# A graph network with residual layernorm: nested Ifs for unused units, a ring of six in the first row stage, and the layernorm chunks spread over five stages

## The chip, the cores and the metric

One core of a Trainium2 chip. The metric is the device time of one launch in microseconds (us), the median of several runs.

## The reference

Inputs: `x` (50000 rows of 128), `src` and `dst` (25000 edges, sorted by `dst`), `edge_attr_16` (25000 by 16), four weight matrices and biases. A layer of edge convolution is `segment_sum(concat(h[src], edge_attr) @ W + b, dst) / max(count, 1)`; layer k takes the concatenated outputs of all layers before it as `h`:

```python
h = _edge_conv(x, src, dst, edge_attr, W0, b0, denom)
outputs = [h]
for W, b in ((W1, b1), (W2, b2), (W3, b3)):
    cat = jnp.concatenate(outputs, axis=1)
    outputs.append(_edge_conv(cat, src, dst, edge_attr, W, b, denom))
x = _layernorm(x + outputs[-1], axis=-1)
```

## The kernel before

The work is linear, so the kernel first sums the rows of `x` over the edges of each destination (a "rank"), 128 edges at a time, and then multiplies the sums once with products of the weights (the product steps, L1234 to L1247 on VectorE, L1709 to L1716 on TensorE, at most `CIT` = 25 steps of 8 blocks). Results are written to `z_of_nodes` for the final sum and to two tables in memory, `h_rows` and `part_rows`. Only a part of the ranks has sources that are themselves destinations; those are listed, and the higher layers are computed for the listed ranks alone:

- **A round** (`round_`, three of them) goes over the list of sources in groups of two blocks of 128: GpSimd gathers two blocks of rows (L674), VectorE builds one-hot matrices (L1407, in `EC`, memory of its own for six groups), TensorE multiplies (L1749, L1755), VectorE adds the result to `UT` (L1423, L1424). GpSimd may be 12 blocks ahead.
- **The first row stage** (`first_rows`) goes over the listed ranks in pairs of blocks. For a pair GpSimd gathers two blocks of 2 KB rows of `part_rows` (L688, "wide"), VectorE casts the node numbers out of them (L1466), makes the pair's rows (L1470 to L1472), GpSimd gathers the nodes' rows of `x` (L666), VectorE adds them (L1459, `add_x`), SyncE stores the parts (L501) and the rows (L496). Pairs share a ring of three places in `SX`: `gather_wide(q)` waits for the rows and the part store of pair q-3. `XLAG` = 1: the node gather of pair q is issued after the wide gather of pair q+1.
- **The second row stage** (`second_rows`) loads the parts back in batches of ten blocks (L515) and makes rows from them (L1486); **the last** (`last_rows`) does so once more, normalises and scatters the rows to the output (L711).

How many blocks there are depends on the input. The rounds' blocks are cut into nine units at `RUNITS` = 0, 60, 66, 70, 76, ..., the rows' at `LUNITS` = 0, 20, 40, 50, 60, 70, ...; unit 0 always runs, and each other one stands in an If of its own on every engine, one behind the other. At the end of a row unit GpSimd and SyncE wait until the last three part stores have landed.

The layernorm of all nodes is 30 **chunks** of 13 rows per partition: SyncE loads a chunk of `x` and one of `z_of_nodes` (L466, L469) into rings of three and two, VectorE adds them and takes statistics (L1386, L1371 to L1379), and, for the chunk before, the scale and shift (L1392, L1393); ScalarE scales (L862) and stores. `load_chunk(c)` waits for the store of chunk c-3. Each transfer is 832 KB (852 thousand bytes), three to a chunk. `LROUND` = 10, 10, 10 puts ten chunks into the first unit (30 groups) of each round, at the groups that `spread_chunks` gives (1, 4, 7, ...); `LSTAGE` = 0, 0 puts none into the row stages. Each engine's order is written out by hand.

Of the kernel before, what the change touches and what calls it, by code (L numbers as in the profile page):

```python
# [7 lines left out]
T = (E + P - 1) // P  # L8
# [38 lines left out]
LROUND = (None, 10, 10, 10)  # L47
LSTAGE = (None, 0, 0)
# [24 lines left out]
AX = mybir.AxisListType  # L73

# [29 lines left out]
def gnn_kernel(nc, x, dst_t, prev_t, src_t, dst_rows, ea, wt, wr, vt, v3, part_of_block, unit_table, out):  # L104
# [11 lines left out]
    with ExitStack() as ctx:  # L116
# [14 lines left out]
        LG = SX[:, :].rearrange("p (j w) -> p j w", w=4 * D)  # L131
        LROWS = SX[:, 0:2 * LB * D].rearrange("p (b j c) -> p b j c", b=2, c=D)
# [176 lines left out]
        wide_here = [sem(f"wide_here{j}") for j in range(3)]  # L309
        x_here, parts_out = ([sem(f"{n}{j}") for j in range(3)] for n in ("x_here", "parts_out"))  # L310
# [45 lines left out]
        def _(e):  # L356
# [122 lines left out]
            def l_pairs(body, tail=None):  # L479
                for u in range(NU):  # L480
                    def unit():
                        for q in range(LUNITS[u] // 2, LUNITS[u + 1] // 2):
                            body(q)
                        if tail:
                            tail(LUNITS[u + 1] // 2)
                    if u:
                        with e.If(n_l > u):
                            unit()
                    else:
                        unit()  # L490
# [7 lines left out]
            def first_pair(q):  # L498
                r = q % 3
                e.wait_ge(s["z_added"], q + 1)  # L500
                e.dma_start(plrows[:, 2 * q:2 * q + 2, :], LG[:, 2 * r:2 * r + 2, D:3 * D]).then_inc(parts_out[r], 16)  # L501
                if 2 * q not in LUNITS:
                    store_rows(1, q - 1)
                if q in SPLACE[1]:
                    chunk(SBASE[1] + SPLACE[1].index(q))

            def first_end(q):
                store_rows(1, q - 1)
                for p in range(q - 3, q):
                    e.wait_ge(parts_out[p % 3], 16 * (p // 3 + 1))  # L510
# [6 lines left out]
            def l_batches(part, here, done):  # L517
                for u in range(NU):
                    lo, hi = LUNITS[u] // LB, (LUNITS[u + 1] + LB - 1) // LB
                    def unit():  # L520
                        for t in range(lo, hi):
                            done(t, min((t + 1) * LB, T) // 2)
                            if t + 2 < hi:
                                load_batch(t + 2, part, here)
                            for w in range(u + 1, NU):
                                if LUNITS[w] <= (t + 2) * LB < LUNITS[w + 1]:
                                    with e.If(n_l > w):
                                        load_batch(t + 2, part, here)
                    if u:
                        with e.If(n_l > u):  # L530
                            unit()
                    else:
                        unit()
# [31 lines left out]
        def _(e):  # L565
# [72 lines left out]
            for i in range(CIT):  # L638
                with e.If(n_s > i):
                    for b in (0, 1):  # L640
# [4 lines left out]
                        for j in range(CG):  # L645
                            c = q * CG + j
                            g.indirect_dma_start(ZF, bass.IndirectOffsetOnAxis(ap=sum_rows[:, c:c + 1], axis=0), HS3[:, b, j, 3 * D + 1:4 * D + 1], None,  # L647
                                                 bounds_check=last_sum, oob_is_err=False).then_inc(scat[b], 16)
            n_e, n_l, n_q = list_counts(e, (UNITS_R, UNITS_L, PAIRS))
# [8 lines left out]
            def gather_x(q):  # L658

                r = q % 3  # L660
                if q >= 3:
                    e.wait_ge(s["z_added"], q - 2)
# [6 lines left out]
            def round_(k, table, last):  # L669
# [7 lines left out]
                for u in range(1, NU):  # L677
                    with e.If(n_e > u):
                        unit(u)

            def gather_wide(q):
                r = q % 3
                if q >= 3:
                    e.wait_ge(rows_made[1], q - 2)
                    e.wait_ge(parts_out[r], 16 * (q // 3))
# [1125 lines left out]
```

## Time and profile before

| | us |
|---|---|
| median of 3 runs (lowest, highest) | 1434.44 (1433.83, 1435.81) |
| the profiled execution | 1429.92 |
| its span | 1427.8 |
| busy: TensorE matmul, VectorE, ScalarE, GpSimd | 564.5, 769.2, 444.0, 802.0 |
| counts of gathers and scatters: L647, L674 (each round), L688, L666, L711 | 144, 70, 60, 60, 60 |
| mean of one scaling on ScalarE, L862 | 0.479 |

The profile is of one execution; its engines' busy times are over the whole span and overlap. The steps priced below are read from stretches of it.

### The profile page before, as it was taken

To read this page: it belongs to the slowest core of one execution; us is meant where nothing else is said; L and a number is where in the kernel's file an instruction comes from. 1 tells how busy PE (TensorE), PEld (TensorE's weight loads), DVE (VectorE), ACT (ScalarE), POOL (GpSimd) and SP (SyncE) were. 2 spreads that over 40 slices of the span, in tenths; PEclk is the share of its full clock that TensorE was granted. 3 is DMA by queue.
4 is the path that set the end of the run, shared out by engine and by line. 5 is a ranking of instruction groups with operands and counts; after the bars stand their busy time and mean duration, and the time that the engine had idled before them with its cause. 6 is when DMAs were issued, how large, how long until landed. Compare 5 with 4: busy or idle time off the path is not lost.

```text
span 1427.8 us, 15526 instructions
## 1 busy us (share of the span) xinstructions
PE 564.5 (40%) x3020; PEld 429.8 (30%) x3020; DVE 769.2 (54%) x2933; ACT 444.0 (31%) x1066; POOL 802.0 (56%) x766
## 2 busy tenths in 40 slices
PE   2454542666657567773544200000254502544000
PEld 1443442444444234442444100000144401544000
DVE  7765557788763533322888321211377745875630
ACT  7543452122323234432355000000144401543440
POOL 6886665245424466666766265655376505663376
PEclk9555665556668888887677555555556666676555
DMA  2667879811105677777677255655657757674311
GB/s 57 230 218 246 295 225 324 257 35 38 27 14 195 203 254 253 245 256 242 240 268 283 73 173 143 179 155 155 179 194 278 273 146 234 249 255 142 117 53 38
DMA packets 157618, 265.66 MB, mean 186 GB/s; under 512 B 22672, under 2 KB 91367, under 8 KB 157472
## 3 DMA queue, kind: packets, MB, share of 16 engines
q1 hardware_dynamic: 112128, 149.57, 31.0%
q0 software_dynamic: 26240, 59.55, 15.3%
q10 hardware_dynamic: 19104, 54.92, 10.1%
q8 instruction: 52, 0.85, 0.3%
q14 instruction: 94, 0.77, 0.2%
HBM read 114.39 MB, written 149.75 MB: 185 GB/s over the span
## 4 chain that ended last, share of the span: by engine, by line
DVE 28%; issue 19%; DMA 19%; PE 14%; POOL 9%; ACT 5%; another core or an unknown queue 2%; SPq 2%; DVEq 2%; POOLq 0%; ACTq 0%
DMA area<-z_of_nodes 5%; DMA SX<-part_rows,nlo 5%; POOL out_rows L711 4%; ACT area L862 3%; DVE stat L1371 3%; DVE area L1199 3%; PE hp L1716 3%; DMA out_rows<-area 2%; DVE area L1386 2%; PE segp L1628 2%; DVE area L1219 2%; DVE area L1125 2%; PE segp L1716 2%; POOL SX L688 2%
## 5 line engine op out<-in xcount | busy, mean ns | idle before, releaser
L631 POOL DMA_INDIRECT G<-x_in,srci x196 | 223.5, 1140 | 157.0 <-PE segp L1628 82.2
L647 POOL DMA_INDIRECT z_of_nodes<-area,sum_rows x144 | 142.0, 986 | 104.6 <-issue 50.5
L1749 PE MATMUL segp<-ZERO 128*128 128x384 f16 (+1 forms) x54 | 26.3, 486 | 352.9 <-DVE EC L1407 335.3
L862 ACT ACTIVATE area<-area,shift,rs 128x128 f32<-128x128 f32 x390 | 153.3, 479 | 21.3 <-DVE shift L1393 19.8
L855 ACT ACTIVATE sd<-dev,eps 128x13 f32<-128x13 f32 x30 | 9.2, 306 | 459.5 <-DVE dev L1379 429.2
L674 POOL DMA_INDIRECT G<-part_rows,s0r x70 | 78.7, 1125 | 87.1 <-DMA part_rows<-UT 50.3
L1749 PEld LDWEIGHTS segp<-ZERO 128*128 128x128 f16 x54 | 6.9, 127 | 357.0 <-DVE EC L1407 338.5
L674 POOL DMA_INDIRECT G<-part_rows,previ x70 | 79.1, 1130 | 51.0 <-issue 36.5
L674 POOL DMA_INDIRECT G<-h_rows,dsti x70 | 78.8, 1126 | 41.6 <-DVE UT L1423 23.4
L688 POOL DMA_INDIRECT SX<-part_rows,nlo x60 | 60.8, 1014 | 70.1 <-issue 28.9
L1755 PE MATMUL segp<-G,EC 128*128 128x128 f32 (+1 forms) x432 | 88.1, 371 | 28.8 <-DMA G<-part_rows,previ 10.3
L1755 PEld LDWEIGHTS segp<-G,EC 128*128 128x128 f32 x432 | 88.0, 287 | 34.0 <-DMA G<-part_rows,previ 12.2
L837 ACT ACTIVATE area<-segp,zero,inv 128x512 f32<-128x512 f32 x72 | 54.4, 776 | 135.0 <-PE segp L1716 56.3
L1628 PEld LDWEIGHTS segp<-SX,G 128*128 128x128 f32 x392 | 91.2, 316 | 11.5 <-ACT SX L778 3.6
L711 POOL DMA_INDIRECT out_rows<-UT,idx x60 | 59.9, 998 | 60.1 <-ACT UT L887 42.1
L1628 PE MATMUL segp<-SX,G 128*128 128x128 f32 x392 | 90.5, 402 | 4.9 <-ACT SX L778 3.2
L789 ACT ACTIVATE UT<-segp,UT 128x1 f32 x56 | 14.6, 261 | 231.2 <-PE segp L1628 191.7
L1755 PEld LDWEIGHTS hp<-G,EC 128*128 128x128 f32 x408 | 83.2, 286 | 6.4 <-issue 2.7
L1755 PE MATMUL hp<-G,EC 128*128 128x128 f32 (+1 forms) x408 | 82.6, 370 | 3.7 <-issue 2.6
L1386 DVE TENSOR_TENSOR area<-area 128x1664 f32<-128x1664 f32 x30 | 56.8, 1894 | 45.5 <-DMA area<-z_of_nodes 41.9
L1371 DVE BATCH_NORM_STATS2 stat<-area 128x6 f32<-128x128 f32 x390 | 78.4, 278 | 1.0
L1466 DVE CAST sum_rows<-SX 128x2 uint32<-128x2 f32 x30 | 6.1, 204 | 129.2 <-DMA SX<-part_rows,nlo 129.2
(392 smaller groups left out, 1608.8 us busy)
## 6 DMA issues: line engine op xcount, KB each, us to landing
part_rows<-area SPq DMA_DIRECT2D x36, 1024.0 KB
z_of_nodes<-ZERO ACTq DMA_DIRECT2D x28, 1024.0 KB
area<-x_in SPq DMA_DIRECT2D x30, 832.0 KB
area<-z_of_nodes SPq DMA_DIRECT2D x30, 832.0 KB
out_rows<-area ACTq DMA_DIRECT2D x30, 832.0 KB
part_rows<-ZERO SPq DMA_DIRECT2D x56, 256.0 KB
h_rows<-area SPq DMA_DIRECT2D x36, 258.0 KB
listed_parts<-SX SPq DMA_DIRECT2D x30, 256.0 KB, 2.6
```

The lines of the kernel that those rows point to most:

```text
L631: g.indirect_dma_start(G[:, slot, 0:D], None, x, bass.IndirectOffsetOnAxis(ap=srci[:, c:c + 1].bitcast(u32), axis=0), bounds_check=last_no ...
L647: g.indirect_dma_start(ZF, bass.IndirectOffsetOnAxis(ap=sum_rows[:, c:c + 1], axis=0), HS3[:, b, j, 3 * D + 1:4 * D + 1], None, bounds_che ...
L674: g.indirect_dma_start(G[:, n % GS, 0:W1 if k == 1 else D], None, table, bass.IndirectOffsetOnAxis(ap=take[k - 1][:, n:n + 1], axis=0), bo ...
L688: g.indirect_dma_start(LG[:, 2 * r + w, :], None, TT, bass.IndirectOffsetOnAxis(ap=wide_row[:, b:b + 1], axis=0), bounds_check=last_row, o ...
L711: g.indirect_dma_start(out, bass.IndirectOffsetOnAxis(ap=node_u[:, b:b + 1], axis=0), UT[:, b * D:(b + 1) * D], None, bounds_check=last_no ...
L837: a.activation(HS3[:, b, j, PARTS], PBANK[j][:, :], ACT.Identity, bias=zero1[:, 0:1], scale=inv[:, g * CG + j:g * CG + j + 1]).then_inc(s[ ...
L862: last = a.activation(XL[:, b, k], XL[:, b, k], ACT.Identity, bias=shift[:, b, r:r + 1], scale=rs[:, b, r:r + 1])
L1371: last = v.bn_stats(stat[cols, b, r, :], src_[cols, r * D:(r + 1) * D])
L1386: lnk(v.tensor_tensor(XL[:, b, :], XL[:, b, :], ZL[:, c % ZRING, :], ALU.add))
L1628: t.matmul(SG[q][:, bass.ds(w, P)], G[:, slot, 0:D], S[:, slot, :], start=False, stop=j == hi - 1).then_inc(s["summed"], 1)
L1716: t.matmul(PBANK[j][:, 0:3 * D], UT[:, (g * CG + j) * P:(g * CG + j + 1) * P], M[:, :], start=False, stop=True).then_inc(s["p_mm"], 1)
L1755: last = t.matmul(bank[:, bass.ds(at_, width)], OH[:, g % OHG, j, w * P:(w + 1) * P], G[:, slot, first:first + width], start=False, stop=j ...
```

## The change

- `nested(e, count, u, end, body)` puts the If of unit u+1 inside that of unit u, behind its body. It takes the place of the rows of Ifs for the round units, row units and product steps on GpSimd, ScalarE, VectorE, TensorE and, for the row units, SyncE. SyncE's counted loop over the product steps stays.
- The first row stage has a ring of six (`WRING`), pairs 3 to 5 of it in `ECS_`, where the one-hots are (`wide_slot`); `XLAG` is 2, and `add_x` follows three pairs behind (`ADDLAG`) instead of one. The semaphores `x_here` are six that the first part of the kernel used, with their count added. VectorE now also waits at a row unit's end for the last six part stores.
- The 30 chunks: 8 in round 1, 4 in the first row stage, 8 in round 2, 2 in the second row stage, 8 in round 3. SyncE issues the loads of a chunk of the first row stage three pairs before VectorE's place for it.

```diff
-LROUND = (None, 10, 10, 10)
-LSTAGE = (None, 0, 0)
+LROUND = (None, 8, 8, 8)
+LSTAGE = (None, 4, 2)
-XLAG = 1
+XLAG = 2
+WRING = 6
+ADDLAG = 3
+def nested(e, count, u, end, body):
+    if u < end:
+        with e.If(count > u):
+            body(u)
+            nested(e, count, u + 1, end, body)
+        LE = ECS_[:, 0:6 * 4 * D].rearrange("p (j w) -> p j w", w=4 * D)
+        wide_slot = lambda r: LG[:, 2 * r:2 * r + 2, :] if r < 3 else LE[:, 2 * r - 6:2 * r - 4, :]
...
+        x_here = [gat[0], gat[1], gat[2], gat[4], gat[5], gat[6]]
+        X_BEFORE = 32 * (UNITS // 2)
...
             def first_pair(q):
-                r = q % 3
+                for i, place in enumerate(SPLACE[1]):
+                    if max(place - ADDLAG, 0) == q:
+                        chunk(SBASE[1] + i)
+                r = q % WRING
                 e.wait_ge(s["z_added"], q + 1)
-                e.dma_start(plrows[:, 2 * q:2 * q + 2, :], LG[:, 2 * r:2 * r + 2, D:3 * D]).then_inc(parts_out[r], 16)
+                e.dma_start(plrows[:, 2 * q:2 * q + 2, :], wide_slot(r)[:, :, D:3 * D]).then_inc(parts_out[r], 16)
                 if 2 * q not in LUNITS:
                     store_rows(1, q - 1)
-                if q in SPLACE[1]:
-                    chunk(SBASE[1] + SPLACE[1].index(q))
...
             def gather_wide(q):
-                r = q % 3
-                if q >= 3:
-                    e.wait_ge(rows_made[1], q - 2)
-                    e.wait_ge(parts_out[r], 16 * (q // 3))
+                r = q % WRING
+                if q >= WRING:
+                    e.wait_ge(rows_made[1], q - WRING + 1)
+                    e.wait_ge(parts_out[r], 16 * (q // WRING))
...
             def l_units(unit):
-                unit(LUNITS[0] // 2, LUNITS[1] // 2)
-                for u in range(1, NU):
-                    with e.If(n_l > u):
-                        unit(LUNITS[u] // 2, LUNITS[u + 1] // 2)
+                own = lambda u: unit(LUNITS[u] // 2, LUNITS[u + 1] // 2)
+                own(0)
+                nested(e, n_l, 1, NU, own)
...
             def first_rows(lo, hi):
-                for q in range(lo, hi + 1):
+                for q in range(lo, hi + ADDLAG):
...
-                    if q > lo:
-                        add_x(q - 1)
+                    if q - ADDLAG >= lo:
+                        add_x(q - ADDLAG)
+                for q in range(hi - WRING, hi):
+                    e.wait_ge(parts_out[q % WRING], 16 * (q // WRING + 1))
+                e.sem_inc(s["tick"], 1)
```

## Rows read from the trace of the kernel before

**Rows 1.** Windows: from:to, us, PE PEld DVE ACT POOL busy (x), PEclk, DMA, GB/s

```profile
666.00:796.00 130.00, 62.30 (x315) 57.53 (x315) 99.73 (x418) 49.05 (x127) 78.89 (x71) 0.69 0.69 241
810.00:874.80 64.80, 0.00 (x0) 0.00 (x0) 16.19 (x72) 0.00 (x0) 40.62 (x40) 0.50 0.57 162
874.80:939.80 65.00, 0.00 (x0) 0.00 (x0) 12.48 (x60) 0.00 (x0) 40.02 (x41) 0.50 0.57 162
939.80:974.40 34.60, 0.00 (x0) 0.00 (x0) 6.37 (x30) 0.00 (x0) 20.18 (x21) 0.50 0.53 152
974.40:1011.30 36.90, 0.00 (x0) 0.00 (x0) 6.50 (x30) 0.00 (x0) 20.25 (x20) 0.50 0.55 141
1156.30:1182.00 25.70, 0.00 (x0) 0.00 (x0) 15.96 (x60) 0.00 (x0) 0.00 (x0) 0.50 0.87 242
1420.50:1427.80 7.30, 0.00 (x0) 0.00 (x0) 0.00 (x0) 0.00 (x0) 0.00 (x0) 0.50 0.00 0
```

**Rows 2.** Timeline of VectorE, chunks: start, us, instruction, [idle before, releaser]

```profile
679.68 1.89 DVE L1386 TENSOR_TENSOR area<-area 128x1664 f32<-128x1664 f32 x1 [12.27 <-DMA area<-z_of_nodes]
...
774.77 1.89 DVE L1386 TENSOR_TENSOR area<-area 128x1664 f32<-128x1664 f32 x1 [1.79 <-DMA area<-z_of_nodes]
...
1017.39 1.89 DVE L1386 TENSOR_TENSOR area<-area 128x1664 f32<-128x1664 f32 x1
...
1052.17 1.88 DVE L1386 TENSOR_TENSOR area<-area 128x1664 f32<-128x1664 f32 x1
...
1117.72 1.89 DVE L1386 TENSOR_TENSOR area<-area 128x1664 f32<-128x1664 f32 x1 [2.07 <-DMA area<-z_of_nodes]
...
1128.01 1.89 DVE L1386 TENSOR_TENSOR area<-area 128x1664 f32<-128x1664 f32 x1 [0.87 <-DMA area<-z_of_nodes]
...
1133.54 0.17 DVE L1393 SCALAR_TENSOR_TENSOR shift<-dev,rs 128x13 f32<-128x13 f32 x1
...
1216.99 1.89 DVE L1386 TENSOR_TENSOR area<-area 128x1664 f32<-128x1664 f32 x1
...
1296.43 1.89 DVE L1386 TENSOR_TENSOR area<-area 128x1664 f32<-128x1664 f32 x1 [3.40 <-issue]
```

**Rows 3.** Chain of waits, VectorE's skips after round 1: start, us, what

```profile
795.76 2.29 issue
...
804.08 3.39 issue
```

**Rows 4.** Chain of waits, GpSimd after the first row stage: landing, longest skip

```profile
1008.82 2.48 DMA listed_parts<-SX
...
1014.88 5.81 issue
```

**Rows 5.** Timeline of VectorE, first instructions after the stages' ends

```profile
807.63 0.29 DVE L1529 TENSOR_TENSOR RX<-RX,RZ 80x128 f32<-80x128 f32 x1 [12.24 <-issue]
...
1014.99 0.26 DVE L1556 TENSOR_SCALAR wlo<-nodec 128x196 f32<-128x196 f32 x1 [6.20 <-issue]
...
1156.23 5.34 DVE L1486 SCALAR_TENSOR_TENSOR UT<-UT,nh,SX 128x128 f32<-128x128 f32 x20 [8.63 <-issue]
...
1326.62 0.24 DVE L1392 RECIPROCAL rs<-sd 128x13 f32<-128x13 f32 x1 [9.54 <-issue]
```

**Rows 6.** Timeline of GpSimd, a unit's end in the first row stage

```profile
860.24 0.99 POOL L688 DMA_INDIRECT SX<-part_rows,nlo  x1 [1.75 <-DVE rela L1472]
...
867.05 1.08 POOL L666 DMA_INDIRECT G<-x_in,sum_rows  x1 [1.91 <-DVE sum_rows L1466]
...
874.82 1.00 POOL L688 DMA_INDIRECT SX<-part_rows,nlo  x1 [5.38 <-issue]
```

**Rows 7.** The page's rates of all DMA, 40 equal slices

```profile
GB/s 57 230 218 246 295 225 324 257 35 38 27 14 195 203 254 253 245 256 242 240 268 283 73 173 143 179 155 155 179 194 278 273 146 234 249 255 142 117 53 38
```

**Rows 8.** Chain of waits, one wide gather and one batch load

```profile
854.89 4.08 DMA SX<-part_rows,nlo
...
1165.45 5.16 DMA SX<-listed_parts
```

More of the change, by code:

```diff
@@ L479, in l_pairs, with unit @@
             def l_pairs(body, tail=None):
[L480 to L486, printed above, removed]
-                        with e.If(n_l > u):
-                            unit()
-                    else:
-                        unit()
+                def unit(u):
+                    for q in range(LUNITS[u] // 2, LUNITS[u + 1] // 2):
+                        body(q)
+                    if tail:
+                        tail(LUNITS[u + 1] // 2)
+                unit(0)
+                nested(e, n_l, 1, NU, unit)
             def store_rows(k, q):
@@ L517, in l_batches, with unit @@
             def l_batches(part, here, done):
-                for u in range(NU):
+                def unit(u):
                     lo, hi = LUNITS[u] // LB, (LUNITS[u + 1] + LB - 1) // LB
[L520 to L533, printed above, removed]
+                    for t in range(lo, hi):
+                        done(t, min((t + 1) * LB, T) // 2)
+                        if t + 2 < hi:
+                            load_batch(t + 2, part, here)
+                        for w in range(u + 1, NU):
+                            if LUNITS[w] <= (t + 2) * LB < LUNITS[w + 1]:
+                                with e.If(n_l > w):
+                                    load_batch(t + 2, part, here)
+                unit(0)
+                nested(e, n_l, 1, NU, unit)
             def second_batch(t, end):
@@ L637, in _, with scatter_step @@
             g.memset(HS3[:, :, :, 4 * D + 3:5 * D + 1], 0.0).then_inc(s["tail_zero"], 1)
-            for i in range(CIT):
-                with e.If(n_s > i):
+            def scatter_step(i):
                     for b in (0, 1):
@@ L893, in _ @@
             l_unit(0)
-            for u in range(1, NU):
-                with e.If(n_l > u):
-                    l_unit(u)
+            nested(e, n_l, 1, NU, l_unit)
         @block.vector
@@ L1352, in _, with step @@
             edge_low(1)
[L1353 to L1360 removed]
+            def step(i):
+                scale_products(i)
+                if i + 2 < CIT:
+                    edge_rest(i + 2)
+                    edge_low(i + 2)
+                else:
+                    e.sem_inc(s["ecs_full"], 1)
+            for i in range(3):
+                with e.If(n_s > i):
+                    step(i)
                 if i == 1:
@@ L1441, in round_ @@
                 unit(0)
-                for u in range(1, NU):
-                    with e.If(n_e > u):
-                        unit(u)
+                nested(e, n_e, 1, NU, unit)
                 e.wait_ge(first_added[k], n_g)
@@ L1449, in l_units @@
             def l_units(unit):
-                unit(LUNITS[0] // 2, LUNITS[1] // 2)
-                for u in range(1, NU):
-                    with e.If(n_l > u):
-                        unit(LUNITS[u] // 2, LUNITS[u + 1] // 2)
+                own = lambda u: unit(LUNITS[u] // 2, LUNITS[u + 1] // 2)
+                own(0)
+                nested(e, n_l, 1, NU, own)
             def add_x(q):
-                r = q % 3
-                e.wait_ge(x_here[r], 32 * (q // 3 + 1))
-                own = LG[:, 2 * r:2 * r + 2, 2 * D:3 * D]
+                r = q % WRING
@@ L1767, in _ @@
                 unit(0)
-                for u in range(1, NU):
-                    with e.If(n_e > u):
-                        unit(u)
+                nested(e, n_e, 1, NU, unit)
 def kernel(x, src, dst, edge_attr_16, L0_gnn_W0, L0_gnn_b0, L0_gnn_W1, L0_gnn_b1, L0_gnn_W2, L0_gnn_b2, L0_gnn_W3, L0_gnn_b3):
```

86 lines of the change are left out of this document (42 added, 44 removed).

## The prediction

> **What bounds the kernel now.** I read the page's table of busy shares first: no engine is over 56% busy, so there is no single bottleneck and each stage has to be priced alone. The table of windows [rows 1] splits the second half of the span: list rounds (the first is its first line), row stages between them, a tail. In the round VectorE is the busiest engine, 99.7 of 130 us, with DMA at 0.69. In the first row stage GpSimd carries it: each unit of ten pairs takes 64.8 or 65.0 us, of which 40 gathers are 40.6 us busy, while VectorE works 16.2 us.
>
> The timeline of VectorE [rows 2] shows what paces a round. Nine gaps between chunks take the 95.1 us from 679.68 to 774.77, 10.6 us each, and the last of these chunks begins after a wait for a z load. That is a loop: statistics, ScalarE's scaling of the chunk before, the store, and only then SyncE's load into the freed buffer. Between two chunks stand three groups of the round.
>
> The chain of waits [rows 3, 4] shows the third thing: the gaps between stages. After round 1 VectorE does nothing from 795.8 to 807.5 us but pass the If of each of the six units that this input does not use; four of those jumps are long, 2.3 to 3.4 us, the first and the last are shown. GpSimd does the same after the first row stage, 5.8 us for the longest. VectorE's own rows [rows 5] give 12.2 us for this end and 6.2, 8.6 and 9.5 us for the others.
>
> **The change part by part.** (By the counts of gathers and scatters on the page, 70, 60 and 144, the input runs 3 of 9 round units, 4 of 9 row units and 18 of 25 product steps.)
>
> *Nested units.* Six or five skipped Ifs in a row become one jump to the end. One long jump is 2.3 to 3.4 us on VectorE and up to 5.8 us on GpSimd [rows 3, 4]; with the 0.5 us before it I put 3.3 us. At the five places that lie on the chain:
> - end of round 1: 12.2 us [rows 5] becomes 3.3, minus 9. VectorE's index work before the first wide gather moves up with it; GpSimd issued its last gather of the round before that and has nothing else to wait for.
> - end of the first row stage: GpSimd resumes at 1011.3 us, when the last parts have landed, and is past its skips at 1020.7, a microsecond before the first gather of round 2 [rows 4]. With one jump it would be there at 1015. But VectorE is next late: it now also waits for those parts at the end of a unit, then has its one jump (about 3 us) and 1.2 us of index work, so 1015.6. Minus 5.
> - end of round 2, 8.6 us [rows 5]: minus 5.5. End of round 3, 9.5 us: minus 6.
> - after the last scatter the span runs on for 7.3 us with no engine busy [rows 1], part of it landing, part GpSimd's five skips: minus 2.
>
> At the end of the product steps the same saving on VectorE and TensorE is worth nothing: SyncE's loop there is a counted one and is not changed, and the first chunk waits 12.3 us for its z load, until 679.68 [rows 2]. After the second row stage the skipped bodies are short and VectorE shows no gap. Sum: minus 27.5, bounds minus 20 (the jump as long as GpSimd's 5.8 us at three places) and minus 31 (every jump 2.3 us).
> The trace agrees here with the Trainium skill, "Runtime: NRT & Kernel Launch", section "Instruction fetch mechanics": a taken branch to code outside the small window of fetched instructions has to fetch it before anything runs. By that rule the nested jump still pays one fetch, and never none; a sum with the gap gone entirely would be 15 us lower, and I do not take it.
>
> *Rounds with 8 chunks for 10.* In the first unit (30 groups) a chunk now follows every 3.75 groups; the first and last places (groups 1 and 28) stay. If the loop of loads went on setting the pace, a round would lose two chunks of 10.6 us, 21.1 us. If VectorE alone set it, it would lose the work of two chunks, 5.65 us each from L1386 to L1393 (1128.01 to 1133.7, [rows 2]), 11.3 us. The truth lies between, because a gap now holds a chunk and about four groups: 5.65 plus 4 x 1.4 us is 11.3 us (the gap from 1117.72 to 1128.01 less the chunk and the 0.87 us of waiting leaves 3.8 for three groups, 1.3 each; I add a little for the groups that wait on TensorE), a little over 10.6. Round 1: nine gaps are 95.1 us, seven of 11.3 are 79: minus 16. Round 2: the first two gaps (1017.39 to 1052.17, 34.8 us, late gathers and one stall) stay and get 2.5 us more for their extra groups, the other seven (75.8 us, to 1128.01) become five of 11.3: minus 17. Round 3 likewise, the last seven gaps are 79.4 us (1216.99 to 1296.43) and become 56.5: minus 20, of which I take 18 because one stall in it may stay. Sum minus 51, bounds minus 34 and minus 64. GpSimd's 70 gathers at 1.3 us are 91 us, so it does not become the bound of a round of 112.
>
> *First row stage, six pairs in flight.* Removed: the waits for a ring of three, about 1.7 us at every second pair, and 1.9 us before the last node gather of a unit, which comes too soon behind its wide one [rows 6]. With XLAG 2 there are 7.8 us between them, and a wide gather lands in about 4 [rows 8]. What remains is GpSimd's own pace: four indirect DMAs a pair at 1.3 us (1.0 busy and 0.3 between), 5.2 us, and the drain at a unit's end, 5.4 us [rows 6], that the change keeps (both engines wait for all parts). A ten-pair unit so takes 57.4 us for 65.0, a five-pair unit 31.4 for 34.6 (939.8 to 974.4) and, at the end, 34 for 36.9 [rows 1].
> *Four chunks moved in.* All four stand in the first unit (pairs 1, 3, 6, 8). VectorE has room: 4 x 5.65 us beside 16.2 us of work in some 60. What has less is the DMA. The unit moves at 162 GB/s with a share of 0.57 [rows 1], 10.5 MB; four chunks add 4 x 2.56 MB. That makes 20.7 MB in 57 us, 360 GB/s, and no slice of the page's line of GB/s is over 324 [rows 7]. So the DMA ends this unit: 20.7 MB at 300 GB/s (between the 242 of [rows 1] and the 324) is 69 us. I take 68, plus 3 on before. The other units keep minus 7.6, minus 3.2 and minus 2.9. Stage: minus 11. Bounds: minus 25 (the DMA hides, GpSimd's pace alone, and a few drains overlap) and plus 14 (it runs at 260 GB/s, and each chunk's 5.65 us holds back a part store and with it a wide gather).
> The Trainium skill speaks against this part, "DMA: Bandwidth & Descriptors", section "Issuing engines are not separate DMA queues": all queues end on the same 16 engines, so moved loads are not free beside gathers; its table of specifications names about 358 GB/s for HBM per core. By that figure alone, an estimate, the unit would be DMA-bound at 58 us, near GpSimd's 57; no stretch of this trace is that fast, and the sum keeps to the 300.
> Added instructions: a wait of VectorE at each unit's end, behind which only the next unit's first cast is queued, and that needs a wide gather that GpSimd issues after the same landing: nothing. SyncE's chunk loads now stand three pairs early and wait for the store of a chunk; behind them wait part stores. I follow them through: load 10 frees at about 24 us after the stage's start, when the first part is due anyway; so 2 to 3 us, within the above.
>
> *Second row stage, two chunks moved in.* It takes 25.7 us at a DMA share of 0.87 [rows 1], its batch loads 5.2 us each [rows 8]. Two chunks add 5.1 MB, 17 us at 300 GB/s, and 11.3 us of VectorE, which idles for 10 of 26 us. SyncE, at pair 7, waits for the store of a chunk that is scaled only from pair 2 on (5.65 us of VectorE, 13 scalings of 0.48 us by the page's line of L862, and the store's landing), some 14 us later, and holds back the load of the fourth batch. By each count it ends 9 to 17 us later; I take plus 11 (bounds plus 5 and plus 17).
>
> *The rest*: half of the ring in the one-hots' memory, shared semaphores, the other shapes of loops change no instruction on the chain: 0 (bounds minus 1 and plus 2).
>
> Sum: minus 27.5, minus 51, minus 11, plus 11 is minus 78.5. The profiled execution took 1429.9 us, so 1351.4; the median of before is 4.5 us above its profiled one, so about 1356.
>
> **The rivals.**
> 1. *The moved chunks eat the ring's gain.* First stage plus 14, second plus 17, rounds minus 34 because the load loop, VectorE and TensorE's slow groups couple. With the jumps: 1434.4 - 27.5 - 34 + 14 + 17 = 1404; halfway between the forecast and that, 1380, is its likelier time. For: DMA 0.87 in the stretches where only loads run. Against: the rounds' waits before chunks are for loads [rows 2], and these go.
> 2. *Everything overlaps better*: rounds minus 63, first stage minus 22, second plus 6, jumps minus 29: 1326. For: VectorE's own work would allow it. Against: TensorE's granted clock is 0.69 in the round [rows 1], nearer its lower level of 1.2 GHz than 2.4, and groups in series wait for its matmuls.
> 3. *The nested bodies cost a jump when they are entered.* If nesting puts each body out of line, every executed If pays a jump on the engine that walks it. On VectorE that is 15 product steps, 2 entries in each of three rounds and 3 in each of three row stages, 30 entries. At the 3.4 us of the dearest VectorE jump that is 102 us against a gain of 78.5: 1458, slower. It decides from 2.6 us an entry. Against it: now an entered body follows with no gap, and nothing in the source moves it.
> 4. *The change does not do what it says*: nested Ifs leave one jump per level; the jumps' 27.5 us stay, 1383.
>
> **How the numbers follow.** Forecast 0.55; rival 1 0.2; rival 2 0.12; rival 4 0.08; rival 3 0.05. A change of under 0.2% is what a measurement of this kernel cannot tell from none. Forecast, rivals 1, 2 and 4 are all faster, save a sliver. Faster 0.94, same 0.01, slower 0.05. The likeliest own range is 1340 to 1374; the one for 8 in 10 reaches into rivals 1, 2 and 4: 1328 to 1390.
>
> **What would show it.** The profile after should have: one gap of about 3 us at VectorE at each round's end, and GpSimd starting round 2 within 6 us of the last part landing; chunk starts about 11.3 us apart; rounds of about 99, 113 and 116 us from their first chunk to VectorE's last copy; in the first row stage, gathers with 0.3 us between them except at four drains, the first unit slowest and at 300 GB/s; a second row stage of 37 us. It is wrong if the rounds keep 10.6 us per chunk and lose 21, if the first unit with its chunks is no slower than the second, or if jumps appear inside units.

## The result, and the profile after

The changed kernel takes 1380.35 us, median of four runs (1375.87 to 1380.76); the kernel before takes 1434.13 us (1427.8 to 1435.81) beside it. The ratio is 0.9626, 95% interval 0.959 to 0.9661: 54 us faster, where the forecast was 78 us faster (1356) with a range from 1328 to 1390. The two profiled executions differ by the same 54 us (1429.92 and 1375.87), so the traces can be set against each other directly.

The page of after (the changed kernel) gives its busy times and two queues of instruction loading (packets, megabytes, share). Busy times hardly move; the gain is in how the work stands together. The instruction queues go from 52 and 94 packets to 39 and 83.

```profile
PE 550.4 (40%) x3020; PEld 417.8 (30%) x3020; DVE 766.2 (56%) x2933; ACT 444.2 (32%) x1066; POOL 798.9 (58%) x766
...
q8 instruction: 39, 0.64, 0.2%
q14 instruction: 83, 0.68, 0.2%
```

VectorE's timeline after, the first instruction behind each stage's end and behind SyncE's wait in the second row stage; they answer to [rows 5], where the same ends cost 12.24, 6.20, 8.63 and 9.54 us.

```profile
783.93 0.29 DVE L1535 TENSOR_TENSOR RX<-RX,RZ 80x128 f32<-80x128 f32 x1 [4.86 <-issue]
...
990.19 0.26 DVE L1562 TENSOR_SCALAR wlo<-nodec 128x196 f32<-128x196 f32 x1 [5.36 <-issue]
...
1111.95 0.35 DVE L1492 SCALAR_TENSOR_TENSOR UT<-UT,nh,SX 128x128 f32<-128x128 f32 x1 [2.67 <-issue]
...
1141.42 0.35 DVE L1492 SCALAR_TENSOR_TENSOR UT<-UT,nh,SX 128x128 f32<-128x128 f32 x1 [10.28 <-DMA SX<-listed_parts]
...
1273.09 0.24 DVE L1397 RECIPROCAL rs<-sd 128x13 f32<-128x13 f32 x1 [2.66 <-issue]
```

The same timeline, the first and the last of the eight chunks of round 1 [rows 2]. They are 82.0 us apart, 11.7 us for each of seven gaps, and the last one waits for no load.

```profile
677.31 1.89 DVE L1391 TENSOR_TENSOR area<-area 128x1664 f32<-128x1664 f32 x1 [14.38 <-DMA area<-z_of_nodes]
...
759.31 1.88 DVE L1391 TENSOR_TENSOR area<-area 128x1664 f32<-128x1664 f32 x1
```

Windows of after: unit 0 of the first row stage whole, two parts of it, units 1 and 2, and last the second row stage from its first chunk on. They answer to [rows 1], where the units took 64.8, 65.0 and 34.6 us.

```profile
786.30:864.70 78.40, 0.00 (x0) 0.00 (x0) 37.26 (x156) 21.64 (x56) 43.73 (x40) 0.50 0.74 243
...
820.00:840.00 20.00, 0.00 (x0) 0.00 (x0) 9.11 (x41) 2.71 (x8) 13.04 (x12) 0.50 0.75 253
840.00:864.70 24.70, 0.00 (x0) 0.00 (x0) 7.82 (x31) 8.12 (x22) 8.60 (x8) 0.50 0.83 283
864.70:922.70 58.00, 0.00 (x0) 0.00 (x0) 12.03 (x60) 0.00 (x0) 40.44 (x41) 0.50 0.63 181
922.70:954.00 31.30, 0.00 (x0) 0.00 (x0) 6.08 (x30) 0.00 (x0) 20.20 (x20) 0.50 0.58 168
...
1114.60:1152.20 37.60, 0.00 (x0) 0.00 (x0) 24.26 (x97) 10.82 (x28) 0.00 (x0) 0.50 0.92 291
```

The balance by stage follows, by VectorE's instructions. Round 1 is taken from its first chunk, the other rounds from the end of the stage before them, to VectorE's last copy; a jump from there to VectorE's next instruction. The times of single units here and below are each from one profiled execution. Unit 0 with its four chunks took 76.1 to 78.7 us in the six runs that have the same four places, so a difference of 1 or 2 us means nothing.

| us | before | after | difference | forecast |
|---|---|---|---|---|
| start of round 1 | 679.7 | 677.3 | -2.4 | 0 |
| round 1 | 115.7 | 101.8 | -13.9 | -16 |
| jump | 12.2 | 4.9 | -7.3 | -9 |
| first row stage, unit 0 | 64.8 | 78.5 | +13.7 | +3 |
| its units 1 and 2 | 99.5 | 89.3 | -10.3 | -10.8 |
| its last unit and the jump | 40.6 | 36.2 | -4.4 | -7.9 |
| round 2 | 132.6 | 119.1 | -13.5 | -17 |
| jump | 8.6 | 2.7 | -5.9 | -5.5 |
| second row stage | 25.9 | 40.3 | +14.4 | +11 |
| round 3 | 134.9 | 118.2 | -16.7 | -18 |
| jump | 9.5 | 2.6 | -6.9 | -6 |
| tail (with the 7.3 us behind the last scatter) | 101.2 | 101.0 | -0.2 | -2 |

The differences sum to -53.4 us, nearly all of the 53.7 by which the spans differ. Of the 25 us missing against the forecast, 11 are in unit 0, 7 in the rounds, 3.5 each in the last unit with its jump and in the second row stage.

One of these lines depends on where it is cut. At the end of the first row stage VectorE is not the engine that round 2 waits for in the kernel before; GpSimd is. These are its first gathers of round 2, before and after:

```profile
1021.68 1.00 POOL L674 DMA_INDIRECT G<-part_rows,previ  x1 [17.10 <-issue]
...
992.38 0.99 POOL L681 DMA_INDIRECT G<-part_rows,previ  x1 [12.37 <-DVEq L1566]
```

Counted to them, the last unit and the jump go from 47.3 to 38.4 us, -9.0 where -7.9 was forecast, and round 2 from there goes from 125.9 to 116.9, -9.0 where -17 was forecast. So the end of the stage came out as forecast, and the 3.5 us belong to the start of round 2.

### The profile page after: what moved, and what is told of

Read it like the earlier page. It is cut to its first block, busy times and chain, and to the rows that moved or that the text cites. A ratio compares the mean times of both kernels' runs of the same rounds, so it can differ in the third digit from the quotient of the medians.

```text
span 1374.1 us, 15435 instructions
## 1 busy us (share of the span) xinstructions
PE 550.4 (40%) x3020; PEld 417.8 (30%) x3020; DVE 766.2 (56%) x2933; ACT 444.2 (32%) x1066; POOL 798.9 (58%) x766
## 3 DMA queue, kind: packets, MB, share of 16 engines
q10 hardware_dynamic: 19104, 54.92, 10.5%
## 4 chain that ended last, share of the span: by engine, by line
DVE 27%; issue 20%; PE 19%; POOL 13%; DMA 12%; ACT 3%; SPq 2%; another core or an unknown queue 2%; DVEq 2%; POOLq 0%; ACTq 0%
POOL out_rows L715 4%; DVE stat L1376 4%; PE hp L1764 4%; PE hp L1722 3%; DVE area L1201 3%; POOL G L638 3%; DVE area L1391 3%; PE segp L1722 3%; POOL G L673 2%; PE segp L1764 2%; DMA area<-src_low_rows 2%; DVE area L1221 2%; DVE area L1127 2%; DMA SX<-part_rows,nlo 2%
## 5 line engine op out<-in xcount | busy, mean ns | idle before, releaser
L638 POOL DMA_INDIRECT G<-x_in,srci x196 | 220.9, 1127 | 158.6 <-PE segp L1634 80.4
L653 POOL DMA_INDIRECT z_of_nodes<-area,sum_rows x144 | 141.8, 985 | 101.8 <-issue 57.4
L1758 PE MATMUL segp<-ZERO 128*128 128x384 f16 (+1 forms) x54 | 21.8, 403 | 352.9 <-DVE EC L1412 332.6
L681 POOL DMA_INDIRECT G<-part_rows,s0r x70 | 75.0, 1072 | 86.8 <-DMA part_rows<-UT 58.2
L681 POOL DMA_INDIRECT G<-part_rows,previ x70 | 76.9, 1098 | 40.2 <-issue 20.0
L1764 PE MATMUL segp<-G,EC 128*128 128x128 f32 (+1 forms) x432 | 76.2, 334 | 21.2 <-DMA G<-part_rows,s0r 8.5
L1764 PEld LDWEIGHTS segp<-G,EC 128*128 128x128 f32 x432 | 74.0, 247 | 24.3 <-DMA G<-part_rows,s0r 8.9
L1722 PE MATMUL hp<-M,UT 128*128 128x384 f32 x144 | 73.6, 599 | 0.0
L673 POOL DMA_INDIRECT G<-x_in,sum_rows x60 | 61.9, 1032 | 18.3 <-issue 17.1
L1391 DVE TENSOR_TENSOR area<-area 128x1664 f32<-128x1664 f32 x30 | 56.7, 1890 | 16.3 <-DMA area<-z_of_nodes 16.1
```

The costliest lines, as they stand in the source:

```text
L638: g.indirect_dma_start(G[:, slot, 0:D], None, x, bass.IndirectOffsetOnAxis(ap=srci[:, c:c + 1].bitcast(u32), axis=0), bounds_check=last_no ...
L673: g.indirect_dma_start(G[:, 2 * r + w, 0:D], None, x, bass.IndirectOffsetOnAxis(ap=node_x[:, b:b + 1], axis=0), bounds_check=last_node, oo ...
L681: g.indirect_dma_start(G[:, n % GS, 0:W1 if k == 1 else D], None, table, bass.IndirectOffsetOnAxis(ap=take[k - 1][:, n:n + 1], axis=0), bo ...
L1391: lnk(v.tensor_tensor(XL[:, b, :], XL[:, b, :], ZL[:, c % ZRING, :], ALU.add))
L1722: t.matmul(PBANK[j][:, 0:3 * D], UT[:, (g * CG + j) * P:(g * CG + j + 1) * P], M[:, :], start=False, stop=True).then_inc(s["p_mm"], 1)
L1764: last = t.matmul(bank[:, bass.ds(at_, width)], OH[:, g % OHG, j, w * P:(w + 1) * P], G[:, slot, first:first + width], start=False, stop=j ...
```

## The experiments

The runs came in four sets, each with the kernel before beside it, and chips differ: the kernel before took 1434.1, 1428.8, 1433.6 and 1395.2 us in the four. So ratios are set against each other within a set, and stages by their own time. The first set is the result above; the second has e1_flat, e2_ring3, e3_chunks10 and e5_nested; the third has e4_store_first, e6_few_bytes, e7_light_stats and e8_no_second; the fourth has the rest.

### The jumps

**e1_flat** undoes the nesting alone.

```diff
-    if u < end:
-        with e.If(count > u):
-            body(u)
-            nested(e, count, u + 1, end, body)
+    for w in range(u, end):
+        with e.If(count > w):
+            body(w)
```

> The changed kernel with the Ifs of the units and product steps one behind the other again; ring of six and chunks 8, 4, 8, 2, 8 stay. Theory A: nesting is worth just the skips seen in the two traces at the ends of stages (7.4 after round 1, 5 after the first row stage, 6.0 and 6.9 after rounds 2 and 3), 25 us: 1405 us. Rival B: nesting also spares fetches elsewhere (24 fewer instruction packets), 35 us or more: 1415. Rival C: another engine hides part of them, 15 us: 1395.

Measured: 1406.26 us against 1428.8 for before, ratio 0.9861 (0.9804 to 0.9917); after's own ratio was 0.9626. The ratios of the two sets are 34 us apart, the medians 26; the spans of the profiled executions are 26.5 us apart, 1400.6 and 1374.1, and 26 of these stand in the gaps at the four ends of stages, as theory A has it. **e5_nested** is the other side: nesting alone, with ring and chunks as before.

```diff
-LROUND = (None, 8, 8, 8)
-LSTAGE = (None, 4, 2)
-XLAG = 2
-WRING = 6
-ADDLAG = 3
+LROUND = (None, 10, 10, 10)
+LSTAGE = (None, 0, 0)
+XLAG = 1
+WRING = 3
+ADDLAG = 1
```

> Nested Ifs alone: ring of three, chunks 10, 0, 10, 0, 10. Theory A: 1434 - 25 = 1409 us, and 20 us over the kernel with the ring of six and no chunks in the row stages. Rival B (nesting spares more fetches): 1400. Rival C (the ring is worth only what units two to four show, 14 us): 1403 or less between them.

Measured: 1401.26 us, ratio 0.98 (0.9758 to 0.9842), so -27.5 us, the forecast's own term; by the interval it could be -23 to -35. That is between theory A and rival B, but the expectations counted from 1434 and the kernel before took 1428.8 here. VectorE's timeline at the end of round 1, of e1_flat and then of e5_nested:

```profile
787.10 0.29 DVE L1534 TENSOR_TENSOR RX<-RX,RZ 80x128 f32<-80x128 f32 x1 [8.99 <-issue]
```

```profile
796.05 0.29 DVE L1535 TENSOR_TENSOR RX<-RX,RZ 80x128 f32<-80x128 f32 x1 [2.77 <-issue]
```

At the ends of rounds 2 and 3 the gap is 10.5 and 10.4 us in e1_flat, 2.7 and 2.7 in e5_nested. At the end of e1_flat's first row stage it is 11.6 us, 2.2 of them the wait for the last parts and the rest skips; in after it is 5.4, with the same 2.2. One jump stays and costs 2.5 to 2.9 us at these ends; rival 4, a jump per level, falls. So does rival 3, a jump for each entered body: e5_nested's rounds (116.5, 131.6, 135.8 us) and units (63.7, 65.6, 35.0 us) are those of before within 1.2 us. At the end of round 1 alone the gap spreads, from 2.5 to 4.9 us over the twelve profiled runs with nested Ifs; why is not shown.

### The ring and the chunks, apart

**e3_chunks10** keeps nesting and the ring and puts all chunks back into the rounds; **e2_ring3** keeps nesting and the moved chunks and has the ring of three.

```diff
# e3_chunks10
-LROUND = (None, 8, 8, 8)
-LSTAGE = (None, 4, 2)
+LROUND = (None, 10, 10, 10)
+LSTAGE = (None, 0, 0)
# e2_ring3
-XLAG = 2
-WRING = 6
-ADDLAG = 3
+XLAG = 1
+WRING = 3
+ADDLAG = 1
```

> The changed kernel with all chunks in the rounds (10, 0, 10, 0, 10); nested Ifs and ring of six stay. Theory A: the rounds take back 44 us, the first unit of the first row stage falls from 78.5 to 58 us and the second row stage from 40 to 26: 1380 + 44 - 21 - 14 = 1389 us. Rival B: the move of the chunks was worth nothing, 1380. Rival C: it was worth what the prediction said for an unhindered first unit, 1400.

> The changed kernel with a ring of three pairs, XLAG 1 and ADDLAG 1; nested Ifs and chunks stay. Theory A: units two to four of the first row stage give back 7.1, 3.3 and 4.0 us, and the first unit, whose part stores land late beside the chunks' transfers, gives back more than 7, so 1400 us or more. Rival B: in the first unit the deep ring bought nothing, since that unit is bound by the bytes: 1394.

Measured, in the set of e5_nested (1401.26): e3_chunks10 1386.3 us, ratio 0.9696 (0.9654 to 0.9738); e2_ring3 1398.14 us, 0.9784 (0.9739 to 0.9829). The ring is worth 15 us without moved chunks, by the stages of the two profiled executions 20, where the forecast had 21. Moving the chunks is worth 3 us with the ring of three, which the intervals don't tell from nothing, and with the ring of six the ratio goes from 0.9696 to 0.9626 (10 us by ratio, 6 by medians of two sets; these intervals overlap too). In unit 0 the deep ring and the chunks work against each other: without chunks it takes 63.7 us with the ring of three and 57.5 with six, with four chunks 80.4 (e2_ring3) and 78.5. So rival B of e2_ring3 had that unit right: the ring buys next to nothing there. Where the chunks' gain goes, by stage, e3_chunks10 to after: rounds -15.4, -12.2, -16.3; unit 0 +21.0; second row stage +16.1. That is 44 won and 37 given back.

GpSimd's timeline of e3_chunks10, the start of unit 0 and of unit 1, and the window of unit 0 (columns as in [rows 1]). Without chunks the unit takes 57.5 us, and the forecast's pace of 57.4 was right.

```profile
797.11 1.00 POOL L693 DMA_INDIRECT SX<-part_rows,nlo  x1 [14.26 <-DVEq L1547]
...
854.66 0.99 POOL L693 DMA_INDIRECT EC<-part_rows,nlo  x1 [5.42 <-issue]
```

```profile
797.10:854.70 57.60, 0.00 (x0) 0.00 (x0) 15.88 (x72) 0.00 (x0) 40.27 (x41) 0.50 0.65 182
```

### What makes unit 0 take 78.5 us

After's chain of waits through unit 0, its DMA pieces and the chunk between two of them:

```profile
790.18 3.71 DMA SX<-part_rows,nlo
...
794.75 1.80 DVE area L1391
796.58 2.62 DVE stat L1376 x13
...
800.40 5.11 ACT area L866 x13
805.53 4.02 DMA out_rows<-area
809.59 0.33 SPq L480
809.97 0.43 SPq L483
810.44 11.16 DMA listed_parts<-SX
...
823.67 7.38 DMA SX<-part_rows,nlo
...
842.67 5.58 DMA EC<-part_rows,nlo
...
850.94 7.16 DMA G<-x_in,sum_rows
...
858.57 5.13 DMA listed_parts<-EC
```

A wide gather lands in 7.4 or 5.6 us where [rows 8] has 4.1, and a part store in 11.2 us where [rows 4] has 2.5. Just ahead of that store the chain names SyncE's wait for a chunk's store (805.53 to 809.55) and its two chunk loads: everything behind them in SyncE's program is late, the part store with them. That gave three theories: the order in SyncE's queue, the bytes, and VectorE's 5.65 us a chunk ahead of a pair's casts. GpSimd's timeline shows where it comes out, a wait for the ring and a drain more than twice as long as in [rows 6]:

```profile
822.37 1.00 POOL L693 DMA_INDIRECT SX<-part_rows,nlo  x1 [8.18 <-DMA listed_parts<-SX]
...
841.21 1.16 POOL L693 DMA_INDIRECT EC<-part_rows,nlo  x1 [2.45 <-DMA listed_parts<-EC]
...
864.75 1.00 POOL L693 DMA_INDIRECT EC<-part_rows,nlo  x1 [12.81 <-issue]
```

**e4_store_first** has SyncE store a pair's part before it waits for a chunk's store and loads.

```diff
-                for i, place in enumerate(SPLACE[1]):
-                    if max(place - ADDLAG, 0) == q:
-                        chunk(SBASE[1] + i)
+                places = SPLACE[1]
+                if q == 0:
+                    chunk(SBASE[1])
...
+                for i, place in enumerate(places):
+                    if i and max(place - ADDLAG - 1, places[i - 1]) == q:
+                        chunk(SBASE[1] + i)
```

> The changed kernel with one difference: in the first row stage SyncE issues the loads of the second, third and fourth chunk behind the part stores of pairs 1, 3 and 6, not ahead of those of pairs 0, 3 and 5. The first unit takes 78.5 us in the changed kernel and 57.5 us with no chunks in it. Theory A (a part store that stands behind a chunk's 1.7 MB in SyncE's queue lands in 11 us instead of 2 to 4 and holds back the wide gather that needs its place): the unit falls to 66 to 70 us and the time to about 1370. Theory B (the 20 MB of the unit take as long in any order): no change, 1380, unit 77 to 79. Theory C (VectorE's four chunks hold the casts back): no change either.

Measured: 1396.34 us against 1433.57, ratio 0.9763 (0.971 to 0.9817), not faster than after. Unit 0 takes 78.7 us, as in after, though the part store on the chain now lands in 4.27 us. Putting the stores first gains nothing, but it doesn't show that the order costs nothing: the chunk loads now stand later, and the chain goes through one of them, for which VectorE waits with the casts behind it. The stall went from the store to the load. The rows are the window, the load on the chain and GpSimd's timeline of e4_store_first, the start of unit 1 last.

```profile
799.80:878.50 78.70, 0.00 (x0) 0.00 (x0) 37.23 (x156) 21.65 (x56) 42.94 (x41) 0.50 0.74 242
```

```profile
846.25 9.73 DMA area<-z_of_nodes
```

```profile
841.91 1.00 POOL L696 DMA_INDIRECT SX<-part_rows,nlo  x1 [3.65 <-DMA listed_parts<-SX]
849.37 1.00 POOL L696 DMA_INDIRECT EC<-part_rows,nlo  x1 [2.56 <-DMA listed_parts<-EC]
862.90 1.76 POOL L676 DMA_INDIRECT G<-x_in,sum_rows  x1 [6.04 <-DVE sum_rows L1472]
878.49 0.99 POOL L696 DMA_INDIRECT EC<-part_rows,nlo  x1 [12.53 <-issue]
```

**e6_few_bytes** takes the bytes away: same instructions and waits, but the chunks in the stage move one row of 13 per partition. **e7_light_stats** keeps the bytes and takes VectorE's time away: their add and statistics are of one row of 13.

```diff
# e6_few_bytes: loads (SyncE); the store on ScalarE likewise, with c - 1
+                w = D if SBASE[1] < c <= SBASE[1] + LSTAGE[1] else LR * D
-                e.dma_start(XL[:, b, :], xv[c]).then_inc(ld_xz[b], 16)
+                e.dma_start(XL[:, b, 0:w], xv[c][:, 0:w]).then_inc(ld_xz[b], 16)
... (the load of z_of_nodes the same way)
# e7_light_stats
+                n = 1 if SBASE[1] <= c < SBASE[1] + LSTAGE[1] else LR
... (the add, on n rows)
-                row_stats(b, LR, al, XL[:, b, :]).then_inc(s["ln_stat"], 1)
+                row_stats(b, n, al, XL[:, b, :]).then_inc(s["ln_stat"], 1)
```

> The changed kernel, but the four chunk loads and four chunk stores that fall into the first row stage move one of their 13 rows (the other rows are left out of the output and of the input); every instruction and wait stays. Theory B (bytes): the first unit falls from 78.5 to about 58 us, the time to 1360. Theory A: also, since the queue ahead of the part stores is empty: 58 to 60. Theory C (VectorE's 5.65 us a chunk, 23 us in all, holds casts back): 70 us or more.

> The changed kernel, but VectorE adds and takes statistics of one of the 13 rows of each of the four chunks in the first row stage (the other rows' values are left wrong), so a chunk takes it under 2 us instead of 5.65; all bytes move. Theory C: the first unit falls to 65 us or less, the time to 1367. Theories A and B: 75 us or more, 1378 or more; A a little less, as the waits for the chunk before end 3.7 us earlier.

Measured: e6_few_bytes 1376.51 us, ratio 0.9599 (0.9554 to 0.9643); e7_light_stats 1399.47 us, ratio 0.9759 (0.9712 to 0.9806); two runs each. Whole times are blurred by the part ahead of round 1 (its start is at 684.3 and 698.1 us), so the stage decides. Windows of unit 0, of e6_few_bytes and then of e7_light_stats:

```profile
797.50:860.90 63.40, 0.00 (x0) 0.00 (x0) 37.26 (x156) 21.65 (x56) 44.99 (x40) 0.50 0.61 176
```

```profile
811.30:883.60 72.30, 0.00 (x0) 0.00 (x0) 21.59 (x108) 21.65 (x56) 40.21 (x41) 0.50 0.79 263
```

No single theory fits: 63.4 us is above the 58 to 60 of A and B and below C's 70, and 72.3 is between C's 65 and the 75 of the others. Against 78.5 in after and 78.7 in e4_store_first, the bytes are worth 15 us and VectorE's work 6; the sum is the whole distance to the 57.5 us of a unit without chunks. Both were at work. The 15 us hold all that goes with the bytes, SyncE's waits for the chunks' stores too; the runs don't split them further. Nor do the bytes set a time by their average rate: the same bytes ran at 263 GB/s in e7_light_stats and at 243 in after, and the second row stage shows 291. But the chunks' transfers come in bursts, and inside these the DMA engines are full. The rows are the DMA's busy share in 40 slices of unit 0 (2 us and 1.4 us each; 9 is 90% or more) and the part stores out of `SX`, with the median time to landing in us last, first of after and then of e3_chunks10:

```profile
DMA  0766713634797999998999940658398799999960
listed_parts<-SX SPq DMA_DIRECT2D x6, 256.0 KB, 11.1
...
DMA  0757776146418953687497369948855893789865
listed_parts<-SX SPq DMA_DIRECT2D x6, 256.0 KB, 2.7
```

In 17 of 40 slices the engines are at 90% or more with the chunks, in 6 without, and the transfers of the dependent chain (gather, cast, gather, add, store) land later.

### How many chunks belong where

The last set, with after once more, had before at 1395.18 us (1392.06 to 1399.64). **e8_no_second** belongs to the set before it: e4's order and chunks 8, 4, 9, 0, 9.

```diff
# chunks in round 1, first row stage, round 2, second row stage, round 3
-LROUND = (None, 8, 8, 8)
-LSTAGE = (None, 4, 2)
+LROUND = (None, 8, 9, 9)     # e8_no_second (with e4's order), e9_849
+LSTAGE = (None, 4, 0)
+LROUND = (None, 9, 9, 9)     # e10_939
+LSTAGE = (None, 3, 0)
+LROUND = (None, 9, 9, 10)    # e12_92910
+LSTAGE = (None, 2, 0)
```

> As the kernel with the stores first, and the two chunks of the second row stage go back to rounds 2 and 3: chunks 8, 4, 9, 0, 9. In the traces so far a chunk in a round costs 6.1 to 8.2 us and one in the second row stage 8 us. Theory: 1 us at most from the kernel with the stores first, about 1369, or 1379 if that one does not move. Rival (VectorE alone would pace the rounds, 5.65 us a chunk, as the prediction's lower bound): 5 us less than that kernel.

> The changed kernel itself once more, beside the others of this call, since the second set of kernels started its rounds 7 to 21 us later in the span than the first, before any edit of theirs. If that is the chip, this kernel does so too on such a chip and its stages from the first chunk on take what they took: 101.8, 78.5 and 40.3 us for round 1, the first unit and the second row stage, each within 7, 1 and 1 us. Time 1380 to 1392 us.

> The changed kernel with chunks 8, 4, 9, 0, 9. Theory (the second row stage is bound by its loads and pays 7 to 8 us for a chunk, a round 6): 3 to 8 us less than the changed kernel. Rival (a round pays 8 us for a chunk, as from 8 to 10): no difference.

> The changed kernel with chunks 9, 3, 9, 0, 9. If each chunk of the first unit costs the same 5.2 us (bytes 3.7, VectorE 1.5), it takes 73 us, and round 1 is 6 to 8 us longer: 1 to 3 us more than with 8, 4, 9, 0, 9. Rival (the first three are nearly free and the fourth is what overloads the unit): the unit takes 66 us or less, and the time is 4 us less than with 8, 4, 9, 0, 9.

> The changed kernel with chunks 9, 2, 9, 0, 10. Same 5.2 us a chunk: the first unit 68 us, round 3 back to 134, so 2 to 4 us more than with 9, 3, 9, 0, 9. Rival (two chunks fit beside the gathers): unit 60 us, time 5 us less.

| chunks | us (range) | ratio (95%) | unit 0 | second row stage |
|---|---|---|---|---|
| 8,4,9,0,9 with e4's order (e4 itself: 1396.34) | 1386.68 (1384.84 to 1390.56) | 0.9665 (0.963 to 0.97) | 76.1 | 24.9 |
| 8,4,8,2,8 (after again) | 1335.08 (1327.39 to 1338.21) | 0.9559 (0.9532 to 0.9586) | 77.5 | 40.5 |
| 8,4,9,0,9 | 1331.29 (1328.89 to 1338.15) | 0.9552 (0.9527 to 0.9576) | 76.9 | 25.2 |
| 9,3,9,0,9 | 1329.11 (1323.63 to 1335.34) | 0.9515 (0.9492 to 0.9538) | 65.2 | 24.9 |
| 9,2,9,0,10 | 1329.04 (1325.62 to 1333.62) | 0.9531 (0.9509 to 0.9553) | 61.9 | 24.5 |

What became of the expectations: after again (r_changed_again) is 45 us below the forecast time, since this chip was faster, but its three stages are 101.1, 77.5 and 40.5 us, as expected. e9_849 is 3.8 us below it by medians, which the ratios don't tell from nothing. e8_no_second is 9.7 us below e4_store_first, more than either guess; between first chunk and tail of the profiled executions it is 3.7. In e10_939 the rival had unit 0 right and the time in part (2.2 us less than e9_849, not 4); in e12_92910 the unit is nearer to the rival's 60 than to 68, but the time doesn't move.

Unit 0 takes 57.5, 61.9, 65.2 and 77.5 us with 0, 2, 3 and 4 chunks: the first three cost 2.6 us each on average, the fourth 12.3. A chunk in round 1 costs 8.3 us (101.1 to 109.4). So in these kernels three belong into the unit, and the fourth doesn't. The window, GpSimd's start of unit 1 and the part stores of unit 0 as above, of e10_939:

```profile
774.00:839.20 65.20, 0.00 (x0) 0.00 (x0) 32.05 (x135) 16.23 (x42) 43.94 (x41) 0.50 0.77 253
```

```profile
839.18 1.00 POOL L693 DMA_INDIRECT EC<-part_rows,nlo  x1 [7.63 <-issue]
```

```profile
listed_parts<-SX SPq DMA_DIRECT2D x6, 256.0 KB, 3.4
```

The ring is never waited for there, the part stores land in 3.4 us for 11.1, and the drain is 7.6 us for 12.8. Full DMA engines alone are not what delays them: here too 17 of 40 slices of the unit (1.6 us each) are at 90% or more. One thing isn't told apart: with four chunks the places are pairs 1, 3, 6, 8 and two chunk loads stand ahead of the first part store in SyncE's program; with three the places are 1, 5, 8 and only one stands there. Number and spacing changed at once, so a fourth chunk at another place stays untested.

In the second row stage two chunks cost 15.3 us (25.2 to 40.5), 7.7 each, and save the rounds 5.1 and 8.7 (round 2: 109.7 and 114.8; round 3: 107.8 and 116.5): nothing won. By stages e10_939 is 1.8 us ahead of after between first chunk and tail, by medians 6 us; their intervals overlap by 0.0006. 9, 3, 9, 0, 9 and 9, 2, 9, 0, 10 are the best kernels that were run, by little, and can't be told apart (1329.11 and 1329.04 us).

## Why the prediction was right in sign and too large in size

- **Nested units, -27.5.** Right: -27.5 alone, +26 when undone. That it fits to the tenth is luck, but the parts fit too: in e5_nested the four ends save 9.5, 5.0, 5.9 and 6.8 us, where 9, 5, 5.5 and 6 were forecast (the second is counted from the last add to GpSimd's first gather of round 2, 12.9 us before and 7.9 in e5_nested). In after the first end saves 7.3, since its jump takes 4.7 us. At the end of the first row stage VectorE's gap of 5.36 us is its wait for the parts and then its jump, as the prediction had it. The tail's -2 was wrong: behind the last scatter stand 7.3 us in both kernels, so skips had no part in it. Round 1 starts 2.4 us earlier in after, but in e1_flat, without nesting, it starts earlier still (676.3 us), so this isn't the work of the nesting. The page "Runtime: NRT & Kernel Launch" of the Trainium skill, section "Instruction fetch mechanics", has a taken branch out of the fetched window pay one fetch. The trace agrees in that one jump is left at each end, of 2.5 to 4.9 us.
- **Rounds, -51.** Measured -44. The mechanism was right: loads no longer set the pace. Before its 30 chunks VectorE now waits 16 us in all, 14.4 of them before the first, where it waited 45.5. The gap between chunks was mis-sized by a little: 11.7 us for 11.3 in round 1, which over seven gaps is 3 us, and 58.3 and 57.3 us for 56.5 over the last five gaps of rounds 2 and 3. The first two gaps of these rounds were forecast to stay and to grow by 2.5 us, to 37.3 and 36.4; they took 38.2 and 40.4. In round 2 this is 5 us more than the prediction's sum allows. Before, 4.3 us of the first gap lay ahead of GpSimd's first gather (1017.39 to 1021.68), and the prediction had booked their going at the end of the stage. They went, but the first gap grew from 19.2 to 26.4 us all the same: the gather that TensorE waits for there lands in 6.3 us where it took 2.6, and behind it stands a stall of 6.3 us whose like stood in the second gap before.
- **First row stage, -11.** Measured about 0 (the last unit, up to its last add, gained 3.6 us); the 11 us are all in unit 0. Units 1 and 2 came out as forecast (57.9 and 31.3 us for 57.4 and 31.4). Unit 0 was forecast as 69 us from 20.7 MB at 300 GB/s and set to 68; it took 78.5 with 19.0 MB at 243. The bytes were counted too high: the load of the unit's second chunk is issued ahead of the unit (774.43 us), so the loads of three chunks and the stores of four fall into it. The failed step is "So the DMA ends this unit": it treated the unit as a pipe at a rate. It is a chain of transfers that wait for one another, and the share of DMA is 0.74 over the unit, full only in bursts. The runs put in its place 57.5 us of GpSimd's pace, 15 for the bytes, which make landings late, and 6 for VectorE's hold on casts. VectorE was put at nothing ("VectorE has room"), by its busy time; what counts is that a pair's cast stands behind 5.65 us of chunk. The bound of plus 14 for the stage named this ("each chunk's 5.65 us holds back a part store") and was the better guess for unit 0 (+13.7), though it was meant for the whole stage. SyncE's wait was foreseen well: the load that should be free 24 us after the stage's start is issued 23.3 us after it (809.59). Whether the order behind it costs the forecast "2 to 3 us" e4_store_first can't tell, since it moved the stall to a load.
- **Second row stage, +11.** Measured +14.4, within the bounds of 5 and 17. SyncE's wait for a chunk's store is there, until it issues the next chunk's loads at 1128.83, but it cost little: the rows that the batch load behind it needs were made only at about 1128.5, behind VectorE's second chunk. What costs is the landing, 10.29 us from 1131.10 beside the chunk's loads where [rows 8] has 5.16, and VectorE idles 10.28 us for it.

```profile
1128.83 0.35 SPq L480 DMA_DIRECT2D area<-x_in  x1
...
1131.10 10.29 DMA SX<-listed_parts
```

- **The rivals.** Rival 1, the moved chunks eat the gain, is the one that came nearest: its likelier time of 1380 is the measured one, though it was a midpoint, and its parts were too dark for the rounds (-34 for -44) and for the first stage (+14 for about 0). That the number fits is luck in good part. Rival 4's 1383 is as near, and its mechanism was absent. Rival 2 fell with the 11.7 us gap, rivals 3 and 4 with e5_nested.
- **The Trainium skill's rule against the change**, from "DMA: Bandwidth & Descriptors", section "Issuing engines are not separate DMA queues", pointed the right way: moved loads aren't free beside gathers, as the landings of 7.4 and 11.2 us show. The rate that the page's section "Specifications" names, about 358 GB/s, gave the prediction's estimate of 58 us for a unit that took 78.5. "No stretch of this trace is that fast" held for the page's slices of 35 us only: in slices of 3.25 us round 1 of the kernel before reaches 411 GB/s.

## What to carry to other kernels

A stage made of dependent transfers has room for foreign work only while landings stay short: ask what each extra megabyte does to the latency of the gather that the next instruction waits for, not whether the sum of bytes fits below a rate. Fill such a stage piece by piece and stop at the knee, here the fourth chunk (at these places), by comparing the price of a piece in each place (2.6 us each for the first three, 12.3 for the fourth, 8.3 in a round). A row of skipped Ifs on every engine is a cost at each stage's end, and nesting them makes it one jump.

## What the runs showed of the hardware beyond that

The kernel before took 1395.2 us on one chip and 1428.8 to 1434.1 in the three other sets, 2.4 to 2.8% more, with the granted clock alike (0.649 to 0.656 on the fast chip, 0.647 to 0.656 in the other sets where it ran beside the experiments). In the changed kernel the difference is in the part ahead of round 1 (its first chunk at 658.9 against 677.3 us) and at the starts of rounds 2 and 3: the second chunk of round 2 follows the first after 15.4 us instead of 26.4, that of round 3 after 18.6 instead of 26.6. In round 2 the chain of after has a stall there that no semaphore in the profile explains, the chain of before has one of 6.13 us, and the chain of r_changed_again has none from round 1 on:

```profile
1008.47 6.25 another core or an unknown queue
```

What it is stays open; no experiment tells it. On such kernels a difference of less than 3% between whole times of different sets says nothing unless the stages bear it out.
